# Decayed keys as two-head stationaries on 32x32 tiles, with orders, stages and PSUM banks chosen anew, in a gated delta-rule block

## What is computed

```python
x = x + 0.5 * ffn(layernorm(x))
x = x + attn(layernorm(x))
x = x + 0.5 * ffn(layernorm(x))

# ffn: token-shifted mixes, r = sigmoid(xr @ W_r), out = r * (relu(xk @ W_k)**2 @ W_v)
# attn: q, k, v = silu(conv4(x @ W)), q and k normalised per head,
#       beta = sigmoid(x @ Wb), g = -exp(A_log) * softplus(x @ Wa + dt_bias)
def step(S, inp):                       # one 16x16 state S for each sequence and head
    qt, kt, vt, gt, bt = inp
    S = S * jnp.exp(gt)[..., None, None]
    pred = jnp.einsum('bhk,bhkv->bhv', kt, S)
    dv = (vt - pred) * bt[..., None]
    S = S + jnp.einsum('bhk,bhv->bhkv', kt, dv)
    ot = jnp.einsum('bhk,bhkv->bhv', qt, S)
    return (S, ot)
# out = (rmsnorm(o) * norm_w * silu(gate)) @ Wo.T
```

## Time and profile before

| | |
|---|---|
| median of 3 runs | 1981.98 us (1980.61 to 1982.77) |
| the profiled execution's own time | 1983.11 us |
| its span | 1981.2 us |
| PE busy | 1810.8 us (91%), 45376 records |
| DVE busy | 1596.2 us (81%) |
| ACT busy | 1034.8 us (52%) |
| POOL busy | 412.9 us (21%) |
| mean granted TensorE clock | 0.943 |

### The profile page before, as it was taken

How to read it: one execution, slowest core, us unless ns; L and a number is a source line. 1 busy time by engine, 2 the same in 40 slices (tenths; PEclk the granted TensorE clock), 3 DMA queues, 4 the chain that set the end, 5 groups by cost and what they waited for, 6 DMA issues and landing times.

```text
span 1981.2 us, 102019 instructions
## 1 busy us (share of the span) xinstructions
PE 1810.8 (91%) x45376; PEld 1517.9 (77%) x45376; DVE 1596.2 (81%) x4326; ACT 1034.8 (52%) x1999; POOL 412.9 (21%) x325
## 2 busy tenths in 40 slices
PE   3778999999999999999999999999999999998886
PEld 2667887878788787878778887878887788787765
DVE  2767898889889888888888888898888889887641
ACT  3545555555555545555555555555555556554322
POOL 0211122222212222222122222122122221221200
PEclk8978999999999999999999999999999999998766
DMA  3000000000000000000000000000000000000000
GB/s 102 1 3 4 14 14 4 14 14 14 14 14 14 9 9 14 14 14 14 14 9 9 14 14 14 14 14 13 4 14 14 14 9 9 9 4 9 8 8 11
DMA packets 21445, 26.24 MB, mean 13 GB/s; under 512 B 2192, under 2 KB 20752, under 8 KB 21008
## 3 DMA queue, kind: packets, MB, share of 16 engines
q1 hardware_dynamic: 21008, 19.73, 3.1%
HBM read 11.33 MB, written 8.39 MB: 10 GB/s over the span
## 4 chain that ended last, share of the span: by engine, by line
PE 77%; DVE 10%; issue 9%; ACT 1%; POOL 0%; DVEq 0%; ACTq 0%; POOLq 0%
PE ps L234 36%; PE ps L216 15%; PE ps L225 9%; PE ps L209 4%; DVE CV L1087 3%; PE ps L402 2%; PE ps L356 2%; PE ps L202 2%; PE ps L560 2%; PE ps L570 2%; PE ps L579 1%; PE ps L372 1%; DVE XR L1364 1%; DVE eg L1344 1%; PE ps L457 1%
## 5 line engine op out<-in xcount | busy, mean ns | idle before, releaser
L1087 DVE SCALAR_TENSOR_TENSOR CV<-ps,cw,CV 128x256 f32<-128x256 f32 x576 | 250.5, 477 | 8.6 <-ACT CV L853 1.8
L234 PE MATMUL ps<-QE,S 64*64 64x16 f32 x4096 | 251.3, 209 | 1.0 <-ACT S L654 1.0
L234 PEld LDWEIGHTS ps<-QE,S 64*64 64x64 f32 x4096 | 209.0, 138 | 55.7 <-issue 54.2
L234 PE MATMUL ps<-WP,V 64*64 64x16 f32 x4096 | 248.9, 208 | 0.0
L234 PEld LDWEIGHTS ps<-WP,V 64*64 64x64 f32 x4096 | 210.0, 138 | 0.0
L234 PE MATMUL ps<-WP,KD 64*64 64x48 f32 x4096 | 147.6, 228 | 25.3 <-issue 23.9
L234 PEld LDWEIGHTS ps<-WP,KD 64*64 64x64 f32 x4096 | 137.5, 143 | 35.2 <-issue 33.8
L988 POOL TENSOR_TENSOR XK<-XK 128x512 f32<-128x512 f32 x32 | 33.5, 1048 | 607.8 <-ACT XK L827 607.8
L1102 DVE TENSOR_TENSOR prod<-A,TZ 128x30 f32<-128x30 f32 (+7 forms) x480 | 140.5, 293 | 13.2
L216 PE MATMUL ps<-w_r_ffn,XR 128*128 128x256 f32 x512 | 139.6, 421 | 9.1 <-DVE XR L1076 6.6
L234 PE MATMUL ps<-KQI,K 64*64 64x48 f32 x4096 | 144.2, 223 | 1.1 <-issue 1.0
(11 more groups left out here) (156 smaller groups left out, 4049.9 us busy)
## 6 DMA issues: line engine op xcount, KB each, us to landing
X<-in_x SPq DMA_DIRECT2D x32, 256.0 KB, 2.7
out_x<-X SPq DMA_DIRECT2D x32, 256.0 KB, 2.1
w_r_ffn<-in_wT_r_ffn SPq DMA_DIRECT2D x1, 256.0 KB, 2.8
w_k_ffn<-in_wT_k_ffn SPq DMA_DIRECT2D x1, 256.0 KB, 3.0
w_v_ffn<-in_wT_v_ffn SPq DMA_DIRECT2D x1, 256.0 KB, 3.8
w_q<-in_wT_q SPq DMA_DIRECT2D x1, 256.0 KB, 4.3
w_k<-in_wT_k SPq DMA_DIRECT2D x1, 256.0 KB, 4.8
w_v<-in_wT_v SPq DMA_DIRECT2D x1, 256.0 KB, 5.0
```

What stands on the lines that cost most here:

```text
L234: last = mm(ps[rows, o:o + n], stat[rows, pk].rearrange("p s c -> p (s c)"), mov[rows], **flags)
L1087: last = stt(d4[:, m], src, cw[:, i, m, tap:tap + 1], d4[:, m], ALU.mult, ALU.add)
```

## The change

`KD4` with four slots becomes `KD2` with two, and `eg4` becomes `eg2`. `pairs` then issues each `d_product` as four matmuls of 32x32 for a pack where it issued two of 64x64. All other forms of matmul stay. With it the order of the stages on PE, DVE, ACT and POOL, the step in which each stands, and the PSUM banks are chosen anew, and with these the waits that guard the banks. SP's stream is the same. The core of the diff:

```diff
-        T2, M2 = (sb(n, [P, PACKS, 2, C]) for n in ("T2", "M2"))
-        K4, KD4, V4, S4 = (sb(n, [P, PACKS, HT, C]) for n in ("K4", "KD4", "V4", "S4"))
+        T2, KD2, M2 = (sb(n, [P, PACKS, 2, C]) for n in ("T2", "KD2", "M2"))
+        K4, V4, S4 = (sb(n, [P, PACKS, HT, C]) for n in ("K4", "V4", "S4"))
...
-        eg4 = sb("eg4", [P, PACKS, HT])
+        eg2 = sb("eg2", [P, PACKS, 2])
...
-                    last = pairs(5 * BANK + i * 3 * C, 3 * C, KD4, pk, WP[g % 2][:, pk], start=True, stop=True)
+                    last = pairs(4 * BANK + i * 3 * C, 3 * C, KD2, pk, WP[g % 2][:, pk], start=True, stop=True)
...
-                tt(eg4[:], along(eg[:], HT), over_packs(slot4[:]), ALU.mult).then_inc(s["eg"], 1)
+                tt(eg2[:], along(eg[:], 2), over_packs(slot), ALU.mult).then_inc(s["eg"], 1)
...
-                tt(KD4[:, rows], vw(k_tok, [3 * C, RING], [0, HT], [1, C]), vw(eg4[:, rows], [HT, RING], [1, HT], [0, C]),
+                tt(KD2[:, rows], vw(k_tok, [3 * C, RING], [0, 2], [1, C]), vw(eg2[:, rows], [2, RING], [1, 2], [0, C]),
                    ALU.mult).then_inc(s["gram_used"], 1)
```

The gate's product and `turn1` now share a bank, as the new head of `turn1` says:

```diff
             def turn1(g):
                 pe.wait_ge(s["xn1"], g + 1)
                 if g:
-                    pe.wait_ge(s["yt"], g)
-                turn(3, XN[0], s["xt1_ps"])
+                    pe.wait_ge(s["gs"], g)
+                turn(5, XN[0], s["xt1_ps"])
```

More of the change, by code:

```diff
@@ L309, in d_product3 @@
[L309 to L327, removed]
@@ L660, in silu_set, with rstd2, o_square @@
                 nc.scalar.preload_act_table_set("silu_and_others")
+            def rstd2(g):
+                act.wait_ge(s["stats2"], g + 1)
+                if g:
+                    act.wait_ge(s["xn2"], g)
+                    act.wait_ge(s["nm2"], g)
+                root(1, s["rstd2"])
+            def o_square(g):
+                act.wait_ge(s["o_ps"], 4 * g + 4)
+                if g:
+                    act.wait_ge(s["ot"], g)
+                af(OSQ[:], bank(6), ACT.Square).then_inc(s["osq"], 1)
@@ new lines, in tap_v @@
+            def tap_v(g):
+                act.wait_ge(s["v_ps"], g + 1)
+                if g:
+                    act.wait_ge(s["vt"], g)
+                d4 = CV[2][:].rearrange("p (m b t) -> p m b t", m=M, b=B)
+                for m in range(M):
+                    o = (0, 1)[m] * BANK
+                    src = ps[:, o:o + B * (CT + TG)].rearrange("p (b t) -> p b t", b=B)[:, :, 0:TG]
+                    last = af(d4[:, m], src, ACT.Copy, scale=cw[:, 2, m, 0:1])
+                last.then_inc(s["tapv"], 1)
@@ new lines, in norm2, with halo_y @@
+            def norm2(g):
+                act.wait_ge(s["nm2"], g + 1)
+                if g:
+                    act.wait_ge(s["yt_ps"], g)
+                for b in range(B):
+                    last = af(XN[1][:, b * H:(b + 1) * H], X[g % NX][:, b, :], ACT.Identity, bias=nmr[:, 1, b:b + 1], scale=rstd[:, 1, b:b + 1])
+                last.then_inc(s["xn2"], 1)
+            def halo_y(g):
+                if g:
+                    act.wait_ge(s["q_ps"], g)
+                    act.wait_ge(s["k_ps"], g)
+                    act.wait_ge(s["v_ps"], g)
+                    act.wait_ge(s["g_ps"], g)
+                    act.wait_ge(s["yt"], g)
+                nc.scalar.copy(Y3[:, :, 0:CT], Y3[:, :, TG:TG + CT]).then_inc(s["haly"], 1)
@@ new lines, in tap_k @@
+            def tap_k(g):
+                act.wait_ge(s["k_ps"], g + 1)
+                if g:
+                    act.wait_ge(s["khat"], g)
+                d4 = CV[1][:].rearrange("p (m b t) -> p m b t", m=M, b=B)
+                for m in range(M):
+                    o = (3, 2)[m] * BANK
+                    src = ps[:, o:o + B * (CT + TG)].rearrange("p (b t) -> p b t", b=B)[:, :, 0:TG]
+                    last = af(d4[:, m], src, ACT.Copy, scale=cw[:, 1, m, 0:1])
+                last.then_inc(s["tapk"], 1)
```

1106 lines of the change are left out of this document (528 added, 578 removed).

## The result

The changed kernel takes 2134.51 us (median of 4 runs, 2123.41 to 2146.19) against 1982.38 us before (4 runs, 1980.61 to 1983.04): a ratio of 1.077, 95% interval 1.0709 to 1.083. It is 152 us slower, and the forecast was 28 us faster, with a range that ended at 2003. The profiled execution took 2123.41 us, with a span of 2121.6.

What follows compares the result with a forecast made beforehand. PE was taken to set the 57.5 us step, DVE 5 us behind. Tiles -1.1, chain +0.4 and normalisation wait -0.3 gave 56.5: 32 us less over 32 steps, 4 more at the ends, so 1954 us, range 1915 to 2003.

Steps and rivals of the forecast that it cites:

- The bound: PE, busy 91% of the span, sets the step of 57.5 us; DVE is 5 us behind and ACT far off.
- a small loss that follows halts: After a halt PE's granted clock drops to 0.50 for a spell, costing some 1 us a step at most.
- The new order of PE: Chain products 1 and 2 back to back lose 0.4 us a step; 0.3 of the third normalisation's wait goes.
- The smaller tiles: In PE's four `d_product`s, 256 records of 32x32 at 11.5 ns save 1.1 us a step (0.3 to 1.6).
- Code supply: PE's halts for instruction code stay at 1.8 us a step (1.0 to 3.5), the dense stretch becoming two lesser ones.
- the second rival: PE's code halts reach 3.0 us a step, one with a spell at 0.50: 1980 us; 0.14, shared with cover.
- The chain: Chain products 1 and 2 back to back on PE wait for DVE's copy: 0.4 us lost a step.
- ACT's tables: Six table loads instead of two add 5.1 us a step on ACT, covered when steady; 4 us booked at the ends.
- The slower rival: DVE's and ACT's queues, from `turn3` to `turn2` or `turn1`, become the bound: 2024 us, or 2003 with half; chance 0.21.
- its sign: PE's waits led by ACT's `XN` or DVE's `M` would show that the slower rival holds.
- The larger gain: On PE, tiles at their lower bound, halts at 1.0 us, fewer slow spells: 83 us less, 1903; chance 0.20.

## Why the prediction was wrong

**The bound was read rightly, one of its terms wrongly.** PE set the step, and does so after. But I treated the clock as a small loss that follows halts ("some 1 us a step at most") and then let it stand unchanged in the sum. The step that failed is the sum of "The new order of PE": it priced each stage at its duration at full clock, so that order could cost only waits, and of these it booked 0.4 us for the chain. The old order against the old order with its `o_products` together shows that order has a price without any wait, 117 us. In the changed kernel the mean clock of the steady part fell from 0.98 to 0.89. By the reckoning above that is up to 5.4 us a step, and PE's waits grew by 1.5, where the sum had 0.1 more (0.4 - 0.3) and nothing for the clock. The order alone, with the old form, costs 126 of the 152 us.

**The smaller tiles.** 64 records take 0.81 us (1007.80 - 1006.99 in the changed kernel's timeline), 12.7 ns each against my 11.5, inside 9.5 to 14.3. That is 3.2 us a step instead of 4.0: 0.8 saved, 1.1 forecast. This size was off by little, but it is not what the form is worth: alone in the old order it cost 46 us.

**Code supply.** I kept 1.8 us a step because the dense stretch was split. In the changed kernel issue at line 234 is 34.3 / 22 = 1.6, so for waits alone that was right, and the upper end of the second rival (3.0) was not reached. What I failed to see is the old order: there the 256 records more cost 1.6 us of halts a step, twice what the tiles save. My second rival had a right mechanism, but its sum was short. 1.2 us more of halts eat the 1.1 of the tiles by themselves, and the spell at 0.50 that it names was priced at nothing, although show 1.9 us for it in `wo` alone.

**The chain.** 0.4 us for the pair back to back was right (0.36 us of waiting at 1020.77). The second wait for `SA`, 1.7 us, was missed: waits for `SA` were to be 0.4 us a step, behind issue, and are 2.0 (44.6 / 22), ahead of it. I had noted that `mix_k3` lies beside a row of POOL's operations and booked nothing; it took 3.24 us for two operations. The exclusive lock in the Trainium skill ("SBUF — State Buffer", Who interferes with whom) agrees with what stands here: DVE's pair ends 0.3 us after POOL's pair.

**ACT's tables.** `turn1` doesn't wait in the steady part, as reckoned, and the loads cost nothing there. At the ends I booked 4 us more. In the profiled executions the six cost some 8 us there, and for the four that were added alone I have no number. But all in all the ends became 19 us shorter, so the sign of that term was wrong for the change as a whole; why is not settled.

**The slower rival** named DVE's and ACT's queues as the bound. DVE's busy time in a step fell to 1084.12 / 22 = 49.3 us of 62.5, so it has 13 us of slack, and PE's waits are led by neither `XN` nor `M`, which was to be its sign. It was right that the change is slower, but by luck, not by its mechanism. One thing in it holds: DVE's queue, with `mix_k3` ahead of a chain copy, does delay PE, and undoing that and the adjacent chain products gained 51 us. It had 0.21 of the chance, and its time ended at 2024. Its sum also took DVE's work as 52.2 us from its three largest waits; the busy time of the earlier trace rows makes it 50.5.

**The larger gain.** Half of its 83 us is 1941, not the 1920 that the prediction gives; the range went by the 1920.

**What stays open.** The three spots that I found and edited account for 61 of the 152 us. Where the others are wasn't settled, nor was any of it split by engine, step or bank. The separations of the `o_products` in the new order gave 17 us at most, where the edit in the old order cost 117. It isn't the same edit: there three quarters stand together, here two. That falls of the clock come back in other dense places is counted above; what each place costs by itself isn't known.

## What to carry to other kernels

Where PE is the bound, read the granted clock by stretches beside the waits, and ask at each fall what PE did before it: a halt, a wait, or small tiles with few columns in a row. In this kernel stages on the whole array between groups of small-tile products are worth more than the waits suggest: two stages moved cost 117 us without a wait, one moved by one place gained 25. And halving the tile here doubled its matmuls, so price such a change in the stretch where it stands, not by its own duration. To tell a halt for code from another, count the instructions from one halt to the next.

## What the runs showed that I had not expected

- The clock falls to its lower level while PE is busy without a gap. In the old order with the `o_products` together it was 0.51 for 13.6 us, and 20 of the 30 falls in 22 steps begin inside an `o_product`.
- The tiles at 32x32 with 48 columns take 12.7 ns a record and still cost 46 us in the old order. Halts for code were up to 2.5 us there, and lie at multiples of 256 of PE's instructions.
- Some 60 us of added work raised the mean clock from 0.875 to 0.906 and took all falls out of the `o_products`.
